# Latent attention: output projection turned and done in two parts per pass, residual sums kept turned in 128-token tiles

## The reference, cut to what matters

```
B, S, D = 16, 100, 512          # batches, tokens of a batch, width;  L = 361 context rows of width 128
x = x + tanh(g_xattn[0]) * L0_xattn(layernorm(x), ctx)      # 16 heads, latent width 128
x = x + tanh(g_ffn[0])   * L0_ffn(layernorm(x))             # signs of the weights, 8-bit activations
x = x + tanh(g_xattn[1]) * L1_xattn(layernorm(x), ctx)
x = x + tanh(g_ffn[1])   * L1_ffn(layernorm(x))             # mixture of experts

# L0_xattn, per head h:
q_big = rope((x @ Wq_h.T) @ w_kc_q_h);  q_r = q_big @ W_qr_h
scores = q_r @ (kv_r @ W_kr_h).T;       ctx_c = softmax(scores) @ kv_r          # kv_r: context rows with rope
out   += (ctx_c @ w_kc_kv_h.T) @ Wo_h.T                                         # the output projection
```

## Time and profile before

| | value |
|---|---|
| median of 3 runs | 1972.14 us |
| profiled execution, own time | 1974.5 us |
| its span, first to last instruction | 1972.2 us |
| start of run 0's first `widen` | 32.0 us |
| last addition to the residual of the first layer, end | 1045.3 us |
| a run of the first layer, 1 to 7 | 60.3 to 67.7 us |
| a run of the first layer, 8 to 15 | 57.8 to 65.6 us |

### The profile page before, as it was taken

The page is one execution under the profiler, slowest core; times in us unless marked ns, Lnnn a source line. Parts: engine busy times, 40 slices in busy tenths (PEclk is TensorE's granted clock), DMA queues, the critical chain, the costliest instruction groups (busy, mean ns, idle before and its releaser), DMA issues. The chain is left out here.

```text
span 1972.2 us, 30321 instructions
## 1 busy us (share of the span) xinstructions
PE 1795.1 (91%) x10844; PEld 1396.3 (71%) x10858; DVE 1332.3 (68%) x2787; ACT 916.3 (46%) x1989; POOL 603.0 (31%) x582
## 2 busy tenths in 40 slices
PE   5899999999999999999995998899977789999997
PEld 4677887778777787777773544566646788888896
DVE  6777677776787778887786896477755643444464
ACT  3444445433543444434443654555444224555563
POOL 5332122331733122331211131232230355343353
PEclk9899999999999999999997999799988899999999
DMA  5022112211121311222016111000014167787773
GB/s 209 17 87 85 58 44 71 87 53 39 56 104 37 121 56 52 99 95 87 26 40 258 35 39 45 18 1 1 1 44 145 38 197 182 261 283 250 252 237 79
DMA packets 51401, 191.77 MB, mean 97 GB/s; under 512 B 7519, under 2 KB 11743, under 8 KB 39991
## 3 DMA queue, kind: packets, MB, share of 16 engines
q1 hardware_dynamic: 41126, 170.14, 24.0%
q0 software_dynamic: 9840, 19.70, 5.3%
q10 hardware_dynamic: 288, 0.00, 0.0%
HBM read 158.29 MB, written 31.51 MB: 96 GB/s over the span
## 5 line engine op out<-in xcount | busy, mean ns | idle before, releaser
L365 POOL TENSOR_TENSOR la_q_roped<-la_q_roped 128x400 f32<-128x400 f32 x128 | 138.0, 1099 | 673.3 <-DVE la_q_roped L827 673.3
L724 ACT ACTIVATE la_probs<-banks,la_minus_max 100x361 f32<-100x361 f32 x256 | 144.7, 565 | 198.6 <-DVE la_minus_max L917 196.6
L827 DVE TENSOR_TENSOR la_q_roped<-banks,la_rope_q 128x400 f32<-128x400 f32 x384 | 196.6, 565 | 21.9 <-PE banks L475 12.0
L529 PEld LDWEIGHTS banks<-identity,la_probs 100*121 100x121 f32 x768 | 113.2, 184 | 72.3 <-DVE la_probs L924 46.6
L924 DVE TENSOR_SCALAR la_probs<-la_probs,la_rsum 100x361 f32<-100x361 f32 x256 | 154.5, 603 | 9.1
L540 PE MATMUL banks<-la_probs_t,la_kv_rows 121*128 121x200 f32 x768 | 151.4, 333 | 0.0
L2189 DVE TENSOR_TENSOR ex_weights_low<-ex_raw_weights,ex_weights_high 128x2048 fp32r<-128x2048 f32 x39 | 89.4, 2293 | 90.7 <-ACT ex_weights_high L2078 89.4
L529 PE MATMUL banks<-identity,la_probs 100*121 100x100 f32 x768 | 126.0, 273 | 22.6 <-DVE la_probs L924 19.2
L917 DVE TENSOR_REDUCE la_minus_max<-banks 100x1 f32<-100x361 f32 x256 | 135.0, 527 | 15.9 <-PE banks L520 9.2
L540 PEld LDWEIGHTS banks<-la_probs_t,la_kv_rows 121*128 121x128 f32 x768 | 131.5, 189 | 1.8
L742 ACT COPY la_probs_t<-banks 121x300 f32<-121x300 f32 x256 | 105.9, 414 | 52.9 <-PE banks L529 52.7
(11 more groups left out here) (375 smaller groups left out, 5057.6 us busy)
## 6 DMA issues: line engine op xcount, KB each, us to landing
ex_raw_weights<-w_exp SPq DMA_DIRECT2D x39, 1024.0 KB
la_weights<-w_pack SPq DMA_DIRECT2D x15, 1856.0 KB, 7.6
residual<-w_exp SPq DMA_DIRECT2D x24, 1024.0 KB
la_kv_turned<-w_ffn SPq DMA_DIRECT2D x30, 384.0 KB, 3.2
la_rope_k<-w_ffn SPq DMA_DIRECT2D x30, 384.0 KB, 3.2
qf_sign_weights<-ffn_signs SPq DMA_DIRECT2D x3, 2048.0 KB, 8.0
ffn_signs<-la_ffn_signs SPq DMA_DIRECT2D x30, 192.0 KB
out<-ex_block_out POOLq DMA_DIRECT2D x13, 256.0 KB
```

The costliest lines, as they stand in the source:

```text
L365: pool.tensor_tensor(roped[:, h, 0, c, :], roped[:, h, 0, c, :], roped[:, h, 1, 1 - c, :], ALU.add).then_inc(b_add, 1)
L529: mm = pe.transpose(ps[0:LC, T_BANK, c * S:(c + 1) * S], prob[:, j % 4, c * LC:(c + 1) * LC], core.ident[0:S, 0:S])
L724: act.activation(prob[:, s % 4, 0:L], ps[0:S, s % 2, 0:L], ACT.Exp, bias=nmax[:, s % 4:s % 4 + 1], accum_out=sums[:, s % 4:s % 4 + 1]).the ...
L827: dve.tensor_tensor(roped[:, h, v, c, :].rearrange("p (b s) -> p b s", b=GB), ps[:, B_BANKS[k % 2], 0:NT].rearrange("p (b s) -> p b s", b=GB),
```

## The change

The output projection is turned. `mh` and `ml` are now the stationary operand (128x128, four blocks k of the 512 features), the context of many tokens the moving one. A run's 800 tokens are cut in two parts at a tile boundary: 384 and 416 tokens in the first half, 352 and 448 in the second. Each part takes four groups of six matmuls (`out(n, run, k)`). The context parts `ctx_high`, `ctx_low` get one buffer for the whole run (it lies where `roped` lies), and the batch that the cut divides is written in two pieces. Part 0 is projected in slots 15 to 18 (13 to 16 in run 7), part 1 in the head of the next run, between its first `widen`s (in run 7 and 15 at the end of the run itself). VectorE's `add` puts each group's result, features on partitions, into `x_all` by tiles: copies in the first run of a half, additions afterwards.

The first two projections of the next run come in slots 6 to 11, three matmuls each, with the last six behind the slots; slots are 20 instead of 23. The two sign pieces of slots 16 to 20 go to slots 8 to 14.

At the end the sums of a tile are turned back (`turn_tile`, four transposes) and added to the input's rows, a new argument `x_rows`, read by DMA as tiles (`finish_tile`). The six tiles of the first half are finished in slots 9 to 11 of runs 8 to 13, with their `bn_stats`; the other seven at the end of run 15. DRAM buffer `x_tokens` with its stores and loads is gone. In the FFN stage `x_quantise(3)` stands ahead of the late tiles' `bn_stats`, and nothing waits for tiles by DMA.

```diff
-        self.packed = (range(0, 6), range(6, 8), range(8, 10), range(10, 11), range(11, PT))
+        self.packed = (range(0, HT // 128), range(HT // 128, PT))
...
-        SCALE_AT, SIGN_AT = (ITEMS, ITEMS + 2), (ITEMS + 2, ITEMS + 4)
-        MIX, OUT = 5, 8
-        SLOTS = OUT + ITEMS - 1
-        AHEAD = (SLOTS - 6, SLOTS - 2)
+        SCALE_AT, SIGN_AT = (8, 13), (9, 14)
+        MIX = 5
+        AHEAD = (17, 21)
+        FIRST_AT = range(6, 6 + KC + KC // 2)
+        TILE_AT = 9
+        OUTS = 2 * KC
+        PIECES = HB + 1
+        TILES0 = HT // 128
...
+        def slots(n):
+            return range(AHEAD[1] + 2 if ends_half(n) else MIX + 2 * HB - 1)
+        def early(n):
+            return n < RUNS and not starts_half(n)
+        def outs_at(n):
+            lo = 13 if ends_half(n) else 15
+            return range(lo, lo + KC)
...
                 for n in range(2, RUNS + 1):
                     refill_sums(n - 1)
                     refill_signs(n - 2, slice(3, None))
+                    if n == PAIRS + 2:
+                        sp.wait_ge(x_t, B)
+                        for t in range(3):
+                            load_tile(t)
+                    if PAIRS + 3 <= n < PAIRS + TILES0:
+                        sp.wait_ge(f_add, n - PAIRS - 2)
+                        load_tile(n - PAIRS)
...
-                    if n == PAIRS + 2:
-                        sp.wait_ge(o_add, PAIRS * HB)
-                        core.store_rows(sp, x_mid, 0)
-                    if n == PAIRS + 3:
-                        core.load_packed(sp, x_mid, 0)
...
+                    else:
+                        pe.wait_ge(o_add, (n - 1) * OUTS + KC)
...
-                def out(n, b):
-                    pe.wait_ge(v_low, n * HB + b + 1)
...
+                def out(n, run, k):
...
                     for h in range(2):
-                        for j, (a, c) in enumerate(((ch, mh), (ch, ml), (cl, mh))):
-                            mm = pe.matmul(ps[0:S, O_BANK, :], a[:, b % 2, h, :], c[:, h, :],
+                        for j, (a, c) in enumerate(((mh, ch), (ml, ch), (mh, cl))):
+                            mm = pe.matmul(ps[:, out_bank(n, run, k), 0:count], a[:, h, kc], c[:, h, :],
                                            start=(h == 0 and j == 0), stop=(h == 1 and j == 2))
...
+                def turn_tile(t):
...
+                    for k in range(KC):
+                        mm = pe.transpose(ps[0:n, tile_bank(t), k * 128:(k + 1) * 128],
+                                          core.x_all[:, t, k * 128:k * 128 + n], core.ident[:])
...
                     widen(n, 0, 0)
+                    if early(n) and n:
+                        out(n - 1, 1, 0)
+                        out(n - 1, 1, 1)
                     widen(n, 0, 1)
+                    if early(n) and n:
+                        out(n - 1, 1, 2)
+                        out(n - 1, 1, 3)
                     project(n, 2, lo)
...
+                        if s == TILE_AT and tile_of(n) is not None:
+                            turn_tile(tile_of(n))
+                        if s in outs_at(n):
+                            out(n, 0, outs_at(n).index(s))
+                        if s in FIRST_AT and early(n + 1):
+                            first_units(n + 1, FIRST_AT.index(s) // KC, [FIRST_AT.index(s) % KC])
...
+                    if ends_half(n):
+                        for k in range(KC):
+                            out(n, 1, k)
+                    elif early(n + 1):
+                        first_units(n + 1, 1, range(KC // 2, KC))
+                    else:
+                        turn_tile(TILES0)
+                        turn_tile(TILES0 + 1)
+                        for k in range(KC):
+                            out(n, 1, k)
+                        for t in range(TILES0 + 2, PT):
+                            turn_tile(t)
...
+                def add(n, run, k):
+                    dve.wait_ge(o_psum, n * OUTS + run * KC + k + 1)
+                    for x, new in delta(n, run, k):
+                        if starts_half(n):
+                            op = dve.tensor_copy(x, new)
+                        else:
+                            op = dve.tensor_tensor(x, x, new, ALU.add)
+                    op.then_inc(o_add, 1)
...
-                    if n == RUNS - 2:
-                        core.wait_packed(dve, 0)
-                        for t in core.packed[0]:
-                            dve.bn_stats(core.stats_all[:, t, :], core.x_all[:, t, :]).then_inc(x_bn, 1)
...
-                core.load_packed(sp, x_mid, 3)
                 sp.dma_start(wq[:, UP, :], w_quant[UP]).then_inc(loaded[UP], 16)
-                core.load_packed(sp, x_mid, 4)
                 sp.dma_start(wq[:, DOWN, :], w_quant[DOWN]).then_inc(loaded[DOWN], 16)
...
+                x_quantise(FIRST - 1)
                 for k in range(1, len(core.packed)):
-                    core.wait_packed(dve, k)
```

More of the change, by code:

```diff
@@ L221, in latent_attention @@
         o_psum, o_add = sem("out_psum"), sem("out_added")
+        f_in, f_last = [sem(f"x_tile_in{i}") for i in range(3)], sem("x_last_tiles_in")
+        f_psum, f_add = sem("x_tile_turned"), sem("x_tile_added")
         q_in = [sem(f"ffn_weights_in{i}") for i in range(2)]
@@ new lines, in tokens_of, with ctx_of, pieces @@
+        def tokens_of(n, run):
+            cut = CUTS[n // PAIRS]
+            return (cut, HT) if run else (0, cut)
+        def ctx_of(n, run, low):
+            lo, hi = tokens_of(n, run)
+            each = 2 * (hi - lo)
+            return ctx_all[:, run, low * each:(low + 1) * each].rearrange("p (h s) -> p h s", h=2)
+        def pieces(n, b):
+            for run in range(2):
+                lo, hi = (max(a, c) for a, c in zip(tokens_of(n, run), (b * S, 0)))
+                hi = min(hi, (b + 1) * S)
+                if lo < hi:
+                    yield run, lo - tokens_of(n, run)[0], slice(lo - b * S, hi - b * S)
@@ new lines, in mixed, with mixed_bank, delta @@
+        def mixed(n, b):
+            return n * PIECES + b + 1 + (b >= CUTS[n // PAIRS] // S)
+        def mixed_bank():
+            return ps[:, V_BANK, 0:2 * S].rearrange("p (h s) -> p h s", h=2)
+        def delta(n, run, k):
+            lo, hi = (v + n // PAIRS * HT for v in tokens_of(n, run))
+            at = lo
+            while at < hi:
+                tile, col = at // 128, at % 128
+                count = max(1, (hi - at) // 128) if col == 0 else 1
+                width = min(128 - col, hi - at)
+                yield (core.x_all[:, tile:tile + count, k * 128 + col:k * 128 + col + width],
+                       ps[:, out_bank(n, run, k), at - lo:at - lo + count * width].rearrange(
+                           "p (t s) -> p t s", t=count))
+                at += count * width
@@ L597, in pair @@
                     wout(n, 1)
-                    for s in range(SLOTS):
+                    for s in slots(n):
                         if s < ITEMS:
@@ L731, in pair @@
                             act.wait_ge(v_psum, n * HB + b + 1)
-                            if b >= 2:
-                                act.wait_ge(o_psum, n * HB + b - 1)
-                            act.copy(ch[:, b % 2, :, :].rearrange("p h s -> p (h s)"),
-                                     ps[:, V_BANK, 0:2 * S]).then_inc(v_high, 1)
+                            for run, at, part in pieces(n, b):
+                                width = part.stop - part.start
+                                act.copy(ctx_of(n, run, 0)[:, :, at:at + width],
+                                         mixed_bank()[:, :, part]).then_inc(v_high, 1)
                         if 2 <= s < ITEMS + 2:
@@ L949, in pair @@
                             chunk(n, 3 + SIGN_AT.index(s))
-                        if s in AHEAD and n + 1 < RUNS:
+                        if ends_half(n) and s in AHEAD:
                             low(n + 1, AHEAD.index(s))
+                        if s == FIRST_AT[KC - 1] + 1 and early(n + 1):
+                            low(n + 1, 0)
+                    if ends_half(n):
+                        for k in range(KC):
+                            add(n, 1, k)
+                    elif early(n + 1):
+                        low(n + 1, 1)
+                    else:
+                        finish_tile(TILES0)
+                        finish_tile(TILES0 + 1)
+                        for k in range(KC):
+                            add(n, 1, k)
+                        for t in range(TILES0 + 2, PT):
+                            finish_tile(t)
                 dve.wait_ge(const_ready, 1)
```

186 lines of the change are left out of this document (125 added, 61 removed).

## The result

The kernel after took 1955.73 us (median of four runs, 1955.51 to 1956.7) against 1973.18 for the kernel before beside it: 0.9907 of the time, 95% interval 0.9892 to 0.9923. So it is faster, by 17.5 us; the forecast was 1941.7, a gain of 30.4. The profiled execution took 1955.5, with a span of 1953.2 (1972.2 before).

What follows compares the result with a forecast made beforehand. TensorE was taken to bound the slots behind slot 5, with VectorE nearly full in second-half heads. The terms summed to -30.4 us, making the median 1941.7, with a range of 1929 to 1960 (the forecast's own: 1932 to 1954).

Steps and rivals of the forecast that it cites:

- (1): Output matmuls: mean width falls from 512 to 400 columns in the stretch TensorE fills, -35.8 us in 16 runs.
- (3): Run boundary: TensorE's first widening waits 0.3 to 0.4 for VectorE's fourth addition, at 14 boundaries, +5.6 us.
- (4): Run heads: four output groups move in, VectorE's additions lie under them; stalls unchanged, 0, bounds -7 to +18 us.
- (7): Run 14's head: statistics of the first six tiles leave VectorE there, -3.1 us.
- (8): Run 10: row stores and tile loads gone, so the signs' wait for a store ends, -1.9 us (0 to -3).
- (5): Thinner slots 6 to 14: nothing in first-half runs, 0.3 a run for seven second-half runs, +2 us, bound +10.
- (6): Run 7's thinned slots: 0 (-3 to +3); its last output groups cover run 8's first wait, -1.3 us.
- (9): End of run 15: waiting for the last additions and finishing the remaining tiles, +2.5 us (0 to +5).
- (10): Boundary to the FFN stage: without tile loads it starts 1.27 behind VectorE's last addition, -2.1 us.
- rival B: Second-half heads' outputs fill TensorE's waits (-7) and the boundary wait is covered (-5.6): 1929 us, chance 0.11.
- Rival A: VectorE becomes the limit in second-half heads and slots 9 to 14: 1959 to 1965 us, chance 0.17.
- Rival D: TensorE's clock falls to 1.2 GHz in thin slots 12 to 14 or run-end waits: slower, 1991 us, chance 0.04.

Runs made afterwards that it cites:

- run 15: Not a follow-up: last of the sixteen runs of the attention loop inside each kernel; slots 6 to end 30.4 us with 400 columns, 34.7 in after once more.
- 400 columns: Kernel before with each output matmul and its addition covering 400 of the 512 columns, so computing less than the reference: 1940.24 us against 1975.13.
- after once more: Kernel after, unchanged, measured and profiled a second time beside the later experiments: 1953.85 us, ratio 0.9900.
- experiment 1: Kernel before with only the output matmuls and their additions narrowed from 512 to 400 columns: 1940.24 us, ratio 0.9832.
- experiment 3: Kernel after with a run's first widening waiting for the third addition of part 0, the second for the fourth: 1946.87 us, ratio 0.9860.
- run 0: Not a follow-up: first of the sixteen runs of the attention loop inside each kernel; the change doesn't touch its head, and no separate time is given.
- the bank edit: Kernel after with the turned probabilities of scores 9 and 11 in bank 7 instead of all in bank 2: 1944.79 us, ratio 0.9856.
- the late sign pieces: Kernel after with a second-half run's two sign pieces in slots 15 and 18 instead of 9 and 14: 1951.03 us, ratio 0.9879.
- the late tile: Kernel after with the tile's transposes, addition and statistics in slots 12 to 14 instead of 9 to 11: 1952.85 us, ratio 0.9891.
- the two edits of run 7: Kernel after with run 7's first four output groups in slots 17 to 20 (1958.03 us), or in 13, 15, 17 and 19 (1952.36 us), instead of 13 to 16.
- run 14: Not a follow-up: a second-half run of the attention loop inside each kernel; its head grew by 1.2 us against the kernel before.

## Why the prediction was right in part

The sign held, and 1955.73 lies inside the stated range of 1929 to 1960. It lies 1.7 above the forecast's own range, and the gain is 17.5 where 30.4 was forecast. That the range held is in part luck: the heads of runs 8 to 15 gave 4.2 more than forecast against the kernel before, and 5.6 more against the one with 400 columns, by a term that had been put at nothing. Without that the time would be 1960 to 1961, at the end of the range or beyond it. Step by step, in us, against the kernel with 400 columns and after once more:

| step | forecast | measured | from |
|---|---|---|---|
| (1) columns | -35.8 | -35.1 | experiment 1 |
| (3) boundary wait | +5.6 | +6.3 | experiment 3 |
| (4), (7), (8) heads of runs 8 to 15 | -5.0 | -10.6 | 148.0 and 171.5, less 34.1 |
| (5) first half, runs 0 to 6 | 0 | +3.6 | slots 6 to end, 205.5 and 180.3, plus 31.9, less 3.1 for (3) |
| (5) with (2), runs 8 to 14 | +4.9 | +13.2 | slots 6 to end, 205.2 and 187.5, plus 34.1, less 3.2 for (3) |
| (6) run 7 and run 8's first matmul | -1.3 | +1.6 | slots 6 to end, 37.4 and 39.0 |
| (9), (10) with (2), run 15 | +3.9 | +4.3 | slots 6 to end, 30.4 and 34.7 |
| (11) FFN | -2.7 | -4.1, -2.5 | TensorE's 200th instruction behind the FFN's first DMA, both profiles |

In the last column 31.9 and 34.1 are seven times the 24 output matmuls that moved from the slots to the next head, by step (4)'s prices. The steps of the attention stage make -27.7 by the forecast and -16.6 by measurement; the stage is 19.2 shorter, and the other 2.6 lie in slots 0 to 5 and run 0's head, which the change doesn't touch. The heads of runs 1 to 7 are as forecast, 32.0 longer.

**Step (1)** held to 0.7 in 35.8, and so did its argument on wide stationary operands: an output matmul of 416 columns with 128 of them starts 0.190 behind the last, which is the 400-column price of 0.183 and 16 x 0.417 ns. The loads themselves did get longer, from 164 to 188 ns, 24 for 28 more columns:

```profile
L553 PEld LDWEIGHTS banks<-la_wout_high,la_ctx_high x2: 164/164/164, 592.0 to 592.7; 128*100 128x100 f32 x2
L645 PEld LDWEIGHTS banks<-la_ctx_parts,la_wout_high x17: 186/188/192, 452.2 to 461.7; 128*128 128x128 f32 x17
```

(one line's instructions, before and after: least, median and most ns). The difference is what the rule of the Trainium skill ("TensorE: Matmul & The Clock Gate", LDWEIGHTS) gives, 23 ns. But between matmuls of 352 or more columns it stays hidden, so the 18 us for exposed loads did not come. Only the first matmul of a group behind a mix or behind transposes stands 0.24 to 0.32 ahead of the second; in the 400-column kernel, with 100 columns to load, these are 0.24 to 0.28.

**Step (5)** is what failed: +13.9 instead of +2 once the tiles' transposes (2.9) are taken out, and beyond its bound of +10. It counted what TensorE and VectorE have to do in slots 12 to 14 and let the two score banks absorb the rest. It did not look at the third resource of the round, the one bank through which the turned probabilities go. The trace of before had it: slot 6 of each run, with neither a mix nor an output group, took 1.12, while slot 7 with a mix took 1.82 and slot 8 with an output group 2.19. That 1.12 is the length of the round, here in run 4:

```profile
320.05 0.56 PE L529 MATMUL banks<-identity,la_probs 100*121 100x100 f32 x3
320.65 0.41 ACT L742 COPY la_probs_t<-banks 121x300 f32<-121x300 f32 x1 [0.39 <-PE banks L529]
321.20 0.53 PE L529 MATMUL banks<-identity,la_probs 100*121 100x100 f32 x3
```

In the second half the same bank turned VectorE's delay of a slot into TensorE's, through ScalarE's order. My bound of +10 for all runs stood for VectorE alone. The prediction's own sign of being wrong, gaps ahead of the transposes, is there: TensorE's waits for ScalarE's copy, us in total, times and longest, in the attention stage before and after,

```profile
PE banks L529 <- ACT la_probs_t L742: 2.1, 4, 0.8
PE banks L606 <- ACT la_probs_t L879: 8.7, 11, 2.1
```

The experiments give the 11.9 back nearly whole: the bank edit 4.7 in the first half and 2.7 in the second, the late sign pieces 2.7, the late tile 1.7, each alone.

**Step (6)** took run 7 for a wash. It asked what the slots lose, not what the groups had been covering: in a run that a chain of ScalarE and VectorE paces, a part of TensorE's work was free (the narrower matmuls won half of their 2.2 there), and half of the groups were moved to where they cost their full length. That is 2.9 us. It is argued from the waits and from experiment 1; the two edits of run 7 did not give it back.

**Step (4)** erred the other way, and for the heads rival B was right. Against the kernel before, run 14's head grew by 1.2 and run 10's by 2.5, where the other five heads of runs 9 to 15 grew by 4.3. So (7) and (8) gave 3.0 and 1.8, nearly their 3.1 and 1.9. Each of the seven heads hid 0.6 of the 4.9 that moved in, which step (4) had put at 0. TensorE's waits for the rope's products from 595 to 1000 us were

```profile
PE banks L475 <- DVE la_q_roped L827: 11.1, 9, 2.4
```

before, and

```profile
PE banks L552 <- DVE la_q_roped L968: 2.3, 6, 0.4
```

after: the new groups stand where TensorE used to wait, as the bound of -7 said, and VectorE's additions fit beside them. Rival A is refuted in the head and half right in slots 9 to 14. Rival B's other half, a covered boundary wait, did not come. Rival D's clock came only on a small scale: it is 1.00 in all rows of the loop above, but ten of the twelve profiles with the new order have one or two short stretches at half clock in run 7 or 8, 1.3 to 1.5 us each where one could be priced, and neither the kernel before nor the 400-column one has any there.

**Steps (9) and (10)**: the last addition ends at 1033.11 and the first DMA starts at 1034.31, 1.2 later (1.3 forecast); run 15 is within 0.4.

## What to carry to other kernels

When work is taken out of a slot, list every buffer and bank whose round passes through the slot, with the engines that hand it on, and compare the longest round with what is left, before counting any engine's load. A slot of the same kind that was already thin, elsewhere in the loop, shows the round's length. And work that leaves a stretch that another engine paces gains little there, but costs its full length wherever TensorE sets the pace.

## What the hardware did that I had not expected

**VectorE stands while GpSimd works.** Two executions of run 3 of the kernel after differ by 1.4 in slots 0 to 5 (13.7 and 12.3). VectorE's scaling of the probabilities takes 0.41 alone. In the first execution two of them took 1.9, under GpSimd's split of the next weights (timeline of VectorE):

```profile
249.11 1.92 DVE L1086 TENSOR_SCALAR la_probs<-la_probs,la_rsum 100x361 f32<-100x361 f32 x1
...
251.57 1.90 DVE L1086 TENSOR_SCALAR la_probs<-la_probs,la_rsum 100x361 f32<-100x361 f32 x1
```

GpSimd at the same time:

```profile
248.93 1.89 POOL L464 TENSOR_TENSOR la_wq_high<-la_weights,zero 128x1024 fp32r<-128x1024 f32 x1 [0.44 <-DMA la_weights<-w_pack]
250.90 2.37 POOL L467 TENSOR_TENSOR la_wq_low<-la_weights,la_wq_high 128x1024 fp32r<-128x1024 f32 x1
```

The first scaling ends at 251.03, behind GpSimd's first part at 250.82, the second at 253.47, behind its second part at 253.27. In the second execution the weights' DMA landed later against the loop (the split starts 26.9 behind the run's first widening instead of 26.3), the two scalings under it took 1.58 and 1.24, and the slots together were 1.4 shorter. That fits the Trainium skill ("SBUF — State Buffer", SBUF: two separate sides): the ports that VectorE and GpSimd share are locked for a whole instruction. Of the 4.8 between the two profiles of one kernel 3.8 lie in slots 0 to 5. That the split is their cause in each of those runs was read in run 3 alone.

**The clock falls in one execution and not in the next.** TensorE pauses for 1.5 and 2.0 in run 7 (waits ahead of 500.72 and 505.91 in after once more) and keeps its full clock; with one wait changed elsewhere the same place reads, in the table of stretches (clock in the third column from the right):

```profile
504.50:506.20 1.70, 1.70 (x9) 1.68 (x8) 0.77 (x3) 1.62 (x5) 1.62 (x3) 0.57 0.00 0
506.20:507.90 1.70, 1.70 (x7) 1.70 (x6) 1.20 (x4) 0.62 (x3) 1.62 (x3) 0.50 0.00 0
507.90:509.60 1.70, 1.70 (x12) 1.70 (x11) 1.03 (x2) 1.09 (x4) 1.62 (x3) 0.93 0.00 0
```

At the lower level of 1.2 GHz run 7 takes 1.3 to 1.5 us more. Of the eight profiles with the output groups of run 7 where after has them, five have this stretch and three don't, with pauses ahead of it that differ by no more than 0.2; what decides is open.
